# First and last 1024 tokens of a Mamba and expert kernel as blocks of 512 tokens, and a new pace between its two loops

## What is computed

```python
h = layernorm(x) * (1 + ca) + sa
val, gate = split(h @ W_in)
val = silu(conv3(val))                      # along the tokens, per channel
B, C = val @ W_B, val @ W_C                 # 16 states each
Delta = softplus((val @ W_delta + delta_base) @ W_tau)
dA = Delta[..., None] * A                   # A = -exp(A_log), 512 channels x 16 states
state = exp(dA) * state + expm1(dA) / (dA + 1e-6) * Delta * B * val    # along the tokens
y = sum over the 16 states of state * C
x = x + ga * ((y * silu(gate)) @ W_out + h)
h = layernorm(x) * (1 + cb) + sb
x = x + gb * (top-2 of 8 experts, each gelu(h @ W1 + b1) @ W2 + b2, and a shared one)
```

## Time and profile before

| what | value |
|---|---|
| median of 3 runs | 5074.86 us (5061.04 to 5090.0) |
| the profiled execution | 5076.93 us |
| its span, first to last instruction | 5075.1 us |
| busy: DVE, ACT, PE, POOL | 82%, 79%, 77%, 74% |
| first scan | 286.8 us |
| DMA | 1104.28 MB, mean 218 GB/s |

### The profile page before, as it was taken

One profiled execution on the slowest core, in us unless ns is written; L12 is line 12 of the kernel. 1 busy time (PEld: TensorE's weight loads), 2 busy tenths in 40 slices (PEclk: granted clock), 3 DMA queues, 4 the chain that ended last, 5 costly groups with the idle time before them and its releaser, 6 DMA issues.

```text
span 5075.1 us, 36705 instructions
## 1 busy us (share of the span) xinstructions
PE 3917.0 (77%) x9708; PEld 1636.1 (32%) x9708; DVE 4160.2 (82%) x3798; ACT 3989.1 (79%) x4187; POOL 3740.0 (74%) x2292
## 2 busy tenths in 40 slices
PE   6441242888888988888898888898888876778989
PEld 3210010333333333333333333333333323333443
DVE  1277899989899999999898989999999989998110
ACT  2386788898899898988898988889899887887111
POOL 0189997787888887887888887888888797888101
PEclk8775565899999999898999999899999887879989
DMA  4589887788888888888888888888888887777322
GB/s 133 140 270 272 256 232 201 216 237 232 231 257 216 260 237 231 227 234 234 229 240 228 257 217 256 228 242 224 230 255 223 225 226 201 220 206 217 101 91 74
DMA packets 365658, 1104.28 MB, mean 218 GB/s; under 512 B 42501, under 2 KB 45445, under 8 KB 358150
## 3 DMA queue, kind: packets, MB, share of 16 engines
q1 hardware_dynamic: 274314, 799.91, 45.7%
q0 software_dynamic: 91136, 302.03, 30.9%
HBM read 673.29 MB, written 160.06 MB: 164 GB/s over the span
## 4 chain that ended last, share of the span: by engine, by line
PE 17%; issue 17%; ACT 17%; DMA 17%; POOL 16%; DVE 13%; SPq 0%; POOLq 0%; DVEq 0%; ACTq 0%
DMA ysum<-hs 12%; PE ps L1024 5%; PE ps L1040 5%; POOL inv L1302 4%; POOL hs L1279 4%; ACT inv L680 3%; DVE ps L1072 3%; DVE ps L1078 3%; PE ps L994 2%; DVE ps L1085 2%; ACT inv L675 2%; POOL ysum L1289 2%; ACT th L687 1%; ACT inv L685 1%; POOL hid L1319 1%
## 5 line engine op out<-in xcount | busy, mean ns | idle before, releaser
L1302 POOL TENSOR_TENSOR inv<-inv,th 128x1024 f32<-128x1024 f32 x512 | 1279.0, 2498 | 263.7 <-ACT th L687 262.9
L1279 POOL TENSOR_TENSOR hs<-hs,Cb 128x1024 f32<-128x1024 f32 x512 | 1296.7, 2533 | 91.8 <-DVE hs L1102 69.9
L1024 PE MATMUL ps<-hf,w1r 128*128 128x512 f32 x2304 | 1139.8, 649 | 55.0 <-ACT xn L760 30.4
L1051 PE MATMUL ps<-Brow,pick 48*128 48x512 bf16 x1024 | 355.1, 431 | 780.9 <-DVE hs L1102 776.1
L1040 PE MATMUL ps<-w2r,hid 128*128 128x512 f32 x1792 | 833.5, 612 | 1.1 <-issue 1.1
L687 ACT ACTIVATE th<-delta,halfA 128x1024 f32<-128x1024 f32 x512 | 582.7, 1138 | 231.4 <-POOL inv L1302 231.1
L1072 DVE TENSOR_TENSOR ps<-ps,us 128x1024 f32<-128x1024 f32 x512 | 627.7, 1226 | 116.9 <-PE ps L1051 116.6
L1289 POOL DMA_DIRECT2D ysum<-hs x480 | 446.8, 931 | 328.1 <-DMA ysum<-hs 290.5
L1085 DVE SCALAR_TENSOR_TENSOR ps<-ps,coef,inv 128x1024 f32<-128x1024 f32 x512 | 658.2, 1286 | 31.6 <-POOL inv L1302 9.7
L1024 PEld LDWEIGHTS ps<-hf,w1r 128*128 128x128 f32 x2304 | 463.2, 208 | 654.9 <-issue 596.9
L1092 DVE SCALAR_TENSOR_TENSOR ps<-nrd,inv_kappa,ps 128x1024 f32<-128x1024 f32 x512 | 659.0, 1287 | 15.0
(11 more groups left out here) (157 smaller groups left out, 5139.8 us busy)
## 6 DMA issues: line engine op xcount, KB each, us to landing
Cb<-c_rows SPq DMA_DIRECT2D x512, 512.0 KB, 4.7
ysum<-hs POOLq DMA_DIRECT2D x512, 512.0 KB, 5.6
w2r<-w_scaled SPq DMA_DIRECT2D x144, 512.0 KB, 7.0
w1r<-in_W SPq DMA_DIRECT2D x144, 512.0 KB, 6.0
gbc<-expert_gates SPq DMA_DIRECT2D x128, 256.0 KB, 5.5
aw<-in_W_val SPq DMA_DIRECT2D x64, 256.0 KB, 5.1
xa<-in_x SPq DMA_DIRECT2D x32, 512.0 KB, 6.3
h_residual<-hT SPq DMA_DIRECT2D x16, 1024.0 KB, 7.3
```

Source lines behind the costliest of these rows:

```text
L1024: mm = t.matmul(o, w1r[:, n % 2, k, h * P:(h + 1) * P], hf[:, k, :], start=(k == 0), stop=(k == G - 1))
L1279: gp_.tensor_tensor(hs[:, c % 3, :], hs[:, c % 3, :], Cb[:, c % 2, :], ALU.mult).then_inc(hC_done, 1)
L1302: gp_.tensor_tensor(inv[:, c % 6, :], inv[:, c % 6, :], th[:, c % 2, :], ALU.mult).then_inc(thinv_done, 1)
```

## The change

The states no longer stand in blocks of two chunks throughout: chunks 0 and 1, and 14 and 15, are blocks of one chunk (SIZES). Such a block has two units, each of two channel groups side by side: columns 0 to 511 of every state tile are one group, 512 to 1023 the other. Where an instruction has a coefficient by channel (square, tanh, abar, the log in inverse_delta, weight, ratio, scan), it becomes two of 512 columns (`parts`). The others stay one instruction of 1024. There are still 32 units and 512 states.

The steps of fronts and backs (now numbered v = 32 H + r) are no longer tied to the slot t of the state: PACE maps slots to steps piecewise. Slots run from -64 to 575 (640, before 704), steps from -96 to 607 as before.

| slots | steps | steps to a slot |
|---|---|---|
| -64 to -13 | -96 to -45 | 1 |
| -12 to -1 | -44 to -21 | 2 |
| 0 to 47 | -20 to 55 | 1.58 |
| 48 to 63 | 56 to 63 | 0.5 |
| 64 to 447 | 64 to 447 | 1 |
| 448 to 511 | 448 to 543 | 1.5 |
| 512 to 575 | 544 to 607 | 1 |

ACT's nine places of four slots are mapped in the same way (`share_act`). The arrays in DRAM lie by chunk, so rows are 512 tokens; loads of a unit and of C write two halves. The delta load of a block's first unit waits for both halves of the softplus of its last chunk, the B rows come in one DMA a chunk with a semaphore each, and SP issues the load of the gate rows and of a block's first delta behind the steps of its slot and not ahead of them. The fold stays tied to the slots. The core of the diff:

```diff
-    c_d = dram("c_rows", [NK, N, TB])
-    delta_d = dram("delta_rows", [NK, G, P, TB])
+    c_d = dram("c_rows", [NQ, N, T])
+    delta_d = dram("delta_rows", [NQ, G, P, T])
...
+        SIZES = [1, 1] + [2] * 6 + [1, 1]
...
+        def rows_of(d, u):
+            (q, n), i = BLOCKS[BLOCK_OF[u]], u - FIRST_U[BLOCK_OF[u]]
+            return (d[q:q + 2, i] if n == 2 else d[q, 2 * i:2 * i + 2]).rearrange("h p t -> p h t")
+
+        def parts(u):
+            n, i = BLOCKS[BLOCK_OF[u]][1], u - FIRST_U[BLOCK_OF[u]]
+            return [(slice(0, TB), i)] if n == 2 else [(slice(0, T), 2 * i), (slice(T, TB), 2 * i + 1)]
...
+        PACE = [(-2 * WIN, -12, -3 * WIN, -44), (-12, 0, -44, -20), (0, 48, -20, 56), (48, 2 * WIN, 56, 2 * WIN), (2 * WIN, (NQ - 2) * WIN, 2 * WIN, (NQ - 2) * WIN), ((NQ - 2) * WIN, NQ * WIN, (NQ - 2) * WIN, (NQ + 1) * WIN), (NQ * WIN, (NQ + 2) * WIN, (NQ + 1) * WIN, (NQ + 3) * WIN)]
+        SLOTS = range(PACE[0][0], PACE[-1][1])
+
+        def share(t):
+            for t0, t1, v0, v1 in PACE:
+                if t0 <= t < t1:
+                    j, n, m = t - t0, t1 - t0, v1 - v0
+                    return range(v0 + j * m // n, v0 + (j + 1) * m // n)
...
-            if r == 19 and H % 2 and 0 <= (H + 1) // 2 < NK:
-                load_unit(G * ((H + 1) // 2))
...
+        def load_unit(sp, u):
+            sp.wait_ge(st_ln[0], 16 * fronts(u))
+            sp.wait_ge(st_ln[1], 16 * fronts(u))
+            ge(sp, abar_done, N * (u - 1))
+            sp.dma_start(halves(delta[:, u % 2, :]), rows_of(delta_d, u)).then_inc(u_ld[u % 2], 16)
...
+        def sync_slot_end(sp, c):
+            r = c % WIN
+            if r == 19 and starts(c // N + 1):
+                load_unit(sp, c // N + 1)
...
-                s.activation(th[:, c % 2, :], delta[:, u % 2, :], ACT.Tanh,
-                             scale=halfA[:, c % N, u % G:u % G + 1]).then_inc(th_done, 1)
+                for cols, g in parts(u):
+                    ins = s.activation(th[:, c % 2, cols], delta[:, u % 2, cols], ACT.Tanh, scale=halfA[:, c % N, g:g + 1])
+                ins.then_inc(th_done, 1)
...
+                for i in share_act(NP * batch + PLACES.index(place)):
+                    b, j = divmod(i, NP)
+                    act_steps(act, *divmod(b, WIN // 4), PLACES[j])
...
-                    v.tensor_tensor_scan(hs[:, c % 3, :], abar[:, c % 4, :], X(c),
-                                         0.0 if first else carry[:, u % G, c % N:c % N + 1], ALU.mult, ALU.add).then_inc(scan_done, 1)
+                    for cols, g in parts(u):
+                        ins = v.tensor_tensor_scan(hs[:, c % 3, cols], abar[:, c % 4, cols], X(c)[:, cols],
+                                                   0.0 if begins(u) else carry[:, g, c % N:c % N + 1], ALU.mult, ALU.add)
+                    ins.then_inc(scan_done, 1)
+
+            times_weight(c)
+            for H, r in steps_of(c)[:1]:
+                dve_steps(dve, H, r, True)
+            times_ratio(c)
+            times_u(c + 1)
+            scan(c)
+            times_abar(c + 1)
+            for i, (H, r) in enumerate(steps_of(c)):
+                if i:
+                    dve_steps(dve, H, r, True)
+                dve_steps(dve, H, r)
```

More of the change, by code:

```diff
@@ new lines, in at @@
+            def at(place):
+                if batch % 4 == 1 and place in ("logs", 0):
+                    inverse_delta(4 * batch // N + 1, place)
+                for i in share_act(NP * batch + PLACES.index(place)):
+                    b, j = divmod(i, NP)
+                    act_steps(act, *divmod(b, WIN // 4), PLACES[j])
+            at("start")
+            for c in states[0:2]:
+                square(c)
+            at("half squared")
+            for c in states[2:4]:
+                square(c)
@@ L693, in take_t, with act_steps @@
+            at("squared")
+            for c in states[0:2]:
+                log(c)
+            at("half logs")
+            for c in states[2:4]:
+                log(c)
+            at("logs")
+            for i in range(4):
+                if states:
+                    exps(states[i])
+                at(i)
+        def act_steps(act, H, w, place):
+            s = nc.scalar
+            qa, qn, qf, qp = H + 2, H + 3, H - 2, H - 3
             def take_t(q, gs):
@@ L863, in act_window @@
[L863 to L879 removed]
+            if w == 0:
+                if place == "start":
+                    take_val(qa, (0, 1))
+                if place == "logs":
+                    take_val(qa, (2,))
+                if place == 0:
+                    take_val(qa, (3,))
@@ new lines, in act_steps @@
+            if w == 1:
+                if place == "start":
+                    silu_of_u(qa)
+                if place == 3:
+                    take_gate(qa, (0, 1))
+            if w == 2:
+                if place == "squared":
+                    take_gate(qa, (2, 3))
+                if place == "start" and has(qf):
+                    act.wait_ge(f_stat, (TPB + 1) * (qf + 1))
+                    s.activation(rstdF[:, :, 0], momF[:, :, 1], ACT.Sqrt, bias=consts[:, 0:1]).then_inc(f_sqrt, 1)
+                if place == "logs":
+                    silu_of_gate(qa)
+                if place == 2:
+                    take_t2(qf, (0, 1))
+                if place == 3:
+                    take_t2(qf, (2, 3))
+                    softplus_exp(qa, 0)
@@ new lines, in act_steps @@
+            if w == 3:
+                if place == "start":
+                    softplus_exp(qa, 1)
+                if place == "logs":
+                    softplus_ln(qa, 0)
+                if place == "squared" and has(qf):
+                    act.wait_ge(mm_log, qf + 1)
+                    score = ps[:, bank_of["log", qf, 0], 0:TPB * E]
+                    s.activation(score, score, ACT.Sigmoid).then_inc(ev_log, 1)
+                if place == 1:
+                    take_w1(qf, 0)
+                if place == 2:
+                    take_w1(qf, 1)
```

525 lines of the change are left out of this document (257 added, 268 removed).

## The result

The changed kernel takes 5140.5 us (median of 4 runs, 5131.9 to 5153.7) against 5075.2 before: 1.0131 times as long, 95% interval 1.0094 to 1.0167. The forecast was 5037, with a range to 5110. The profiled execution took 5153.7 us (span 5151.8), the slowest of the four, so its stretches add up to some 12 us more than the median would.

The account below looks back on a forecast made before the run. No engine bounds the whole span: VectorE sets the pace of states 480 to 511, TensorE the tail and most of a compressed back. Terms -57 + 49 + 4 + 140 - 176 = -40 gave 5037 us, range 4950 to 5110.

Parts of the forecast that it names:

- Part 1: Before the first scan: states begin earlier, scan 0 at 230 us and not 286.76; -57 us (bounds -45 and -60).
- Part 2: 128 states in one-chunk blocks: split instructions cost VectorE 0.45 us a state (0.3 to 0.6), ACT some 0.6.
- Part 3: First 64 states: added steps and splits make POOL, DVE and ACT about equally full; 617 us, +49 (+15 to +95).
- Part 4: Last 64 states: three backs, not two, with TensorE nearly full; 648 us, +140 (+62 to +183).
- Rivals B and C: Last 64 states: B, VectorE keeps the bound, 4959, chance 0.25; C, ACT's queue waits for TensorE, 5107, chance 0.17.
- Part 5: Tail behind the last state: the first of two windows vanishes, the last stays; -176 us (bounds -170 and -178).
- Part 6: Middle 384 states and DMA queues: same schedule, more 2 KB pieces, gate load behind the steps; +4 us (0 to +20).
- rivals on the slower side: ACT waiting for TensorE in the last states, 5107, chance 0.17; front 1 still ending before scan 0, 5094, chance 0.08.

Follow-up runs that it names:

- no_splits: Changed kernel with DRAM rows of 1024 tokens and delta load waiting for its own half only, split instructions left whole (wrong coefficients): 5010.6 us.
- shared_c: Changed kernel with DRAM rows of 1024 tokens, delta load waiting for its own half, and C row loaded once in one-chunk blocks: 4996.9 us.
- before_c_34k: Kernel before with C rows laid out by chunk and one unused 2 KB row behind each chunk's 16, halves 34 KB apart: 5063.3 us, ratio 0.9985.
- before_c_2k: Kernel before with only the C rows laid out by chunk, so Cb loads move 2 KB rows 32 KB apart: 5184.5 us.
- before_c_pieces: Kernel before with its layout, each Cb load written as two 2 KB halves of one contiguous 4 KB row: 5073.0 us.
- best: Not defined by name; apparently the changed kernel with C rows 34 KB apart, own-half delta wait and one C load in one-chunk blocks: 5002.7 us.

## Why the prediction was wrong

**Part 1, to the first scan.** -48 against -57. Right in kind: the scan of state 0 stands behind take_p of front 1. The last take_p ended at 234.6, not at about 226. I had given ACT's squares and logs ahead of the gate evacuations 3 us. ACT did get to the first evacuation only at 211.1 (198.4 before), but what released PE's last gate matmuls was a DMA: the load of their weights took 11.4 us to land (201.2 to 212.6) where it had taken 5.3, with the DMA engines full between 206.2 and 212.7 (a share of 1.04 as the profile counts it, 411 GB/s). PE stood idle for 6.5 us, its granted clock fell to 0.55 behind that, and the eight matmuls took 6.53 us and not 3.67. Before, then after:

```profile
204.41 3.67 PE L968 MATMUL ps<-hT,aw 128*128 128x512 f32 x8 [0.42 <-DMA aw<-in_W_gate]
```

```profile
212.71 6.53 PE L1047 MATMUL ps<-hT,aw 128*128 128x512 f32 x8 [6.46 <-DMA aw<-in_W_gate]
```

The loads weren't in my sum. The total lies within the bounds given.

**Part 2, the splits.** 0.45 us a state was too much. Two scans of 512 columns take 2.33 us together against 2.28 for one of 1024 (rows 5). The shortest slots take 7.46 us against 7.16 at the start and 7.58 against 7.22 at the end, where the scan reads a carry; no_splits goes back to 7.16 and 7.22. So a state costs 0.30 to 0.36, near the lower bound, and in the total no_splits finds 13 us for all 128 states. The mistake was to price each split by a difference of durations from separate rows: back to back, the second instruction of a pair adds less than that.

```profile
238.39 2.33 DVE L1189 TENSOR_TENSOR_SCAN hs<-abar,ps 128x512 f32<-128x512 f32 x2
```

**Part 3, the first 64 states.** +43 against +49, but that the sum came out is in part luck. It held 28 us for splits (18 and 10), of which no_splits gives back 9. And I put the stretch on three equally full engines. shared_c halves the bytes of the C rows there, with the engines as busy as before, and takes 20 us away: so the DMAs have a part in what bounds it, and my sum had no term for them. The bytes of a C row are the same as in the kernel before (512 KB a state), so the 20 us aren't a cost of the change, and the rest of the +43 isn't divided up by these runs.

**Part 4, the last 64 states.** +132 against +140, TensorE busy 532.61 of 639.1 us (83%; "over 83%" had been said). DVE's wait for the B matmul grew, as announced, from 10.9 us in the two windows to 99.4:

```profile
DVE ps L1155 <- PE ps L1138: 99.4, 32, 7.4
```

The term was right and, in the w1 slots, its mechanism; that freeing them gives back 30 us and not 60 shows that the handoffs between engines, and the clock that falls with PE's work, stand just behind it, which the 95% in my sum covered by luck rather than by knowledge. Rivals B and C both fall: no_splits leaves the last 64 where they were, and ACT's table loads and evacuations cost DVE nothing that the waits show. The 12 and 4 more table loads are there (53 against 41 in the last 64 states, 42 against 38 in the first). The row that I read for the missing drain shows the idle time ahead of a load; behind one it is as small (median 0.01 us of 385 in the kernel before). Two slips in the working: 45.6 + 4 x 0.9 is 49.2 and not 48, which makes three backs 4 us longer; and by C's own formula it makes the whole slower from 19 us a back ((38 + 20) / 3), not from 13, since 20 us are in the sum already.

**Part 5, the tail.** -169 against -176, just outside the bounds of -170 and -178.

**Part 6, the step that failed.** I wrote "+4 (0 to +20)" for the middle, from the packets' number and the DMA share. Two things were missed. First, the layout: I looked at the size of a row, which costs nothing (before_c_34k), and not at the address of the second one. By chunk, the two halves of a C row lie N x T x 4 bytes = 32 KB apart, where they had been one row. Second, the change has a gate load that comes behind the steps and a delta load that waits for both halves, and I followed only the gate load's cover. The wait at slot 19 is for a DMA that POOL issues in slot 20, and SP stands there with the second half of the xa loads and the C rows of two slots queued behind it; it had no term in the sum. It is worth 36 us on the good layout and some 16 on the slow one; the layout is worth 81 to 85. The upper bound, 20 us, had no row behind it.

The rivals on the slower side had been at 5107 at most, and all of them put the loss into the stretches that were rescheduled. None was about the stretch that was only re-addressed.

## What to carry to other kernels

When an edit changes how an array lies in memory, price the addresses as an edit of their own: which rows one transfer reads at once, and how far apart they are; here 32 KB between two rows cost 114 us, and one padded row and one run were enough to find it. A wait put into a DMA queue is priced by what stands behind it in that queue, the rest of the slot's loads too. When matmuls are left out to see what TensorE costs, read the granted clock of the stretch as well: those that remain may run slower, and the test then gives back less than the work was worth. And read the stretch that the change "doesn't touch" with the same care as the others: 384 equal steps turn 0.3 us into 120.

## What the runs showed of the hardware

- Cb loads of 256 packets of 2 KB, out of two rows each read by 128 partitions: rows 32 KB apart cost 114 us over 512 loads (0.22 us each); 34 KB apart they cost nothing (-8, with the interval of the ratio just reaching 1); 2112 bytes apart, and so not aligned to 2 KB, 34 us. Whether the last is from the alignment or from neighbourhood was not tried, nor whether 4, 8 or 16 KB do the same harm as 32.
- The DMA engines' busy share hardly shows it, 0.85 against 0.84 in the middle, since the stretch grows with it. What shows it are the landing times of most of the large transfers, also of those that read elsewhere (before to after: aw 5.1 to 6.6 us, w2r 7.0 to 8.2; not the gates' rows, gbc, 5.5 to 5.6), and the packets: of the 232321 packets of 2 KB on queue q1 the median is 84 ns in before_c_2k and in before_c_34k, but the mean is 111 against 99 and the slowest tenth starts at 173 against 112.
- Packets of 2 KB in place of 4 KB for the C rows, of the same total, cost nothing measurable here (before_c_34k: 5063.3 against 5071.8).
- The halves of one contiguous row, written as two pieces, were moved as packets of 4 KB again (before_c_pieces: 274314 packets, as in the kernel before).
- The granted TensorE clock of the last 64 states fell from 0.89 to 0.78 when 324 matmuls were left out, and PE's busy time fell by 98 us (527.21 to 429.10).
- A multiplication on POOL whose second operand is read twice by a stride of zero is no slower (128 of them in the kernel best, mean 2424 ns, against 2544 for the plain ones there).
- Two instructions of 512 columns on DVE, back to back: STT pairs 1.40 us against 1.29 for one of 1024; scan pairs 2.33 against 2.28, with a carry 2.44 against 2.34.
